# Rows of x, x1 and the adjacency renumbered so that a partition's eight rows are neighbours in memory, a third buffer for the sign masks, and a group's quotients one batch later

## What is computed

```python
x  = layernorm(x + (adj == 1) @ (x @ w1) + (adj == 2) @ (x @ w2) + (adj == 3) @ (x @ w3) + bias)
h  = x @ W.T + b
e  = (h @ we1 + be1) + (h @ we2 + be2).T          # 8192 x 8192
e  = where(e >= 0, e, 0.01 * e)
p  = softmax(where(adj > 0, e, -9e15), axis=1)
x  = layernorm(x + p @ h)
```

## Time and profile before

| | |
|---|---|
| median of 3 runs | 1608.69 us (1608.07 to 1610.11) |
| the profiled execution | 1608.2 us, of which its span is 1606.5 us |
| TensorE busy | 1435.4 us (89%) |
| VectorE busy | 1088.5 us (68%) |
| ScalarE busy | 979.4 us (61%) |
| GpSimd busy | 119.5 us (7%) |
| TensorE's mean granted clock | 0.969 of full |
| read from memory | 296.5 MB |

### The profile page before, as it was taken

How to read it: one execution, slowest core, us unless ns; L and a number is a source line. 1 busy time by engine, 2 the same in 40 slices (tenths; PEclk the granted TensorE clock), 3 DMA queues, 4 the chain that set the end, 5 groups by cost and what they waited for, 6 DMA issues and landing times.

```text
span 1606.5 us, 19366 instructions
## 1 busy us (share of the span) xinstructions
PE 1435.4 (89%) x6934; PEld 668.8 (42%) x6934; DVE 1088.5 (68%) x2432; ACT 979.4 (61%) x1536; POOL 119.5 (7%) x154
## 2 busy tenths in 40 slices
PE   1747798889999999999999988999999989998996
PEld 0323344344444444444444433444444444444443
DVE  3556677867878968778678665666566766666554
ACT  2223535555556556456555467787787887788674
POOL 3101111110101110100101030000000000000000
PEclk9988899899999999999999998999999999999998
DMA  9999999995889879967969121000000001000100
GB/s 117 125 123 118 126 98 118 112 115 69 97 108 98 98 70 121 86 69 96 84 67 115 13 66 40 8 27 27 27 27 27 27 27 52 28 27 27 34 1 15
DMA packets 124164, 109.60 MB, mean 68 GB/s; under 512 B 4960, under 2 KB 115104, under 8 KB 124064
## 3 DMA queue, kind: packets, MB, share of 16 engines
q0 software_dynamic: 67584, 67.12, 45.7%
q1 hardware_dynamic: 56480, 41.20, 9.1%
HBM read 296.49 MB, written 13.14 MB: 193 GB/s over the span
## 4 chain that ended last, share of the span: by engine, by line
PE 56%; ACT 17%; DVE 12%; DMA 11%; issue 4%; SPq 0%; DVEq 0%; ACTq 0%
PE ps L1208 35%; PE ps L1167 18%; ACT neg_masks L991 13%; DMA edges<-x 7%; DVE neg_masks L597 3%; DVE pos_masks L599 2%; DMA x_rows<-x 2%; PE ps L1176 1%; DMA e_scratch<-e_turned 1%; DMA e_row<-e_scratch 1%; PE ps L1222 1%; DVE tables L660 1%; ACT L1049 1%; PE ps L1188 1%; DVE seen L559 1%
## 5 line engine op out<-in xcount | busy, mean ns | idle before, releaser
L991 ACT ACTIVATE neg_masks<-e_row,cols 128x512 int8<-128x512 f32 x1024 | 640.4, 708 | 176.7 <-PE ps L1208 137.6
L1208 PE MATMUL ps<-pos_masks,tables 128*128 128x512 fp8e4 x2048 | 616.1, 383 | 65.6 <-DVE pos_masks L599 55.7
L1208 PE MATMUL ps<-neg_masks,tables 128*128 128x512 fp8e4 x2048 | 615.2, 382 | 0.0
L1167 PE MATMUL ps<-edge_masks,tables 128*128 128x512 fp8e4 (+1 forms) x2048 | 470.7, 389 | 0.0
L1208 PEld LDWEIGHTS ps<-pos_masks,tables 128*128 128x128 f16 x2048 | 197.1, 98 | 322.4 <-issue 93.3
L597 DVE TENSOR_TENSOR neg_masks<-pos_masks,neg_masks 128x2048 uint16<-128x2048 uint16 x128 | 156.9, 1226 | 241.9 <-ACT neg_masks L991 240.5
L1208 PEld LDWEIGHTS ps<-neg_masks,tables 128*128 128x128 f16 x2048 | 201.7, 98 | 246.8 <-issue 8.8
L1167 PEld LDWEIGHTS ps<-edge_masks,tables 128*128 128x128 f16 x2048 | 203.3, 100 | 238.1 <-issue 22.2
L578 DVE TENSOR_SCALAR edge_masks<-edges 128x512 uint16<-128x512 uint16 x512 | 123.5, 307 | 77.6 <-PE ps L1167 77.6
L982 ACT ACTIVATE edges<-ps 128x1024 uint8<-128x1024 bf16 x64 | 65.0, 1016 | 177.1 <-PE ps L1176 177.1
L599 DVE TENSOR_TENSOR pos_masks<-pos_masks,neg_masks 128x2048 uint16<-128x2048 uint16 x128 | 156.8, 1225 | 4.4
(11 more groups left out here) (128 smaller groups left out, 728.5 us busy)
## 6 DMA issues: line engine op xcount, KB each, us to landing
adj_in<-adj POOLq DMA_DIRECT2D x84, 512.0 KB, 12.0
tables<-adj POOLq DMA_DIRECT2D x28, 512.0 KB, 20.9
e_row<-e_scratch SPq DMA_DIRECT2D x34, 256.0 KB, 4.1
edges<-adj POOLq DMA_DIRECT2D x16, 512.0 KB, 12.0
part_scratch<-a_c_rows SPq DMA_DIRECT2D x18, 256.0 KB, 3.3
part_in<-part_scratch SPq DMA_DIRECT2D x18, 256.0 KB, 3.0
edges<-x SPq DMA_DIRECT2D x8, 512.0 KB, 16.2
x_rows<-x SPq DMA_DIRECT2D x8, 512.0 KB, 4.9
```

The source lines that it names most:

```text
L991: ins = e.activation(GN[:, n:n + GR].bitcast(I8), e1row[:, q % 2, :], ACT.Sign, bias=t2[:, JC * c + j:JC * c + j + 1])
L1167: ins = e.matmul(ps[:, h, :], v_hl[:, i, JC * c + j, :], U0[:, n:n + GR].bitcast(kind), start=c == 0 and j == 0 and i == 0, stop=c == NCH ...
L1208: ins = e.matmul(z_bank(q, k), tab[:, c, 2 * k + i, j, :], mask[:, n:n + GR].bitcast(F8A), start=first and j == 0 and i == 0, stop=final a ...
```

## The change

Three things are changed.

**Row numbers.** Before, partition p of a block held rows p, p+128, ..., p+896. After, it holds rows 8p to 8p+7. Loads and stores of x, x1 and the output then move 4 KB (a block) or 2 KB (a group) in one piece for each partition, where they moved 512 B pieces. The adjacency's pieces stay 4 KB in memory and 1 KB in the core, 512 a half; a partition's four rows now lie 32 KB apart and neighbouring partitions 256 KB, where it was 4 MB and 32 KB. To number the columns in the same way, `convert` reads the packed bytes with a step of eight bytes.

**Three gate buffers.** From batch 51 on the gates rotate over three buffers; the third lies in `y_turned`, which is free by then. Gates of batch m then wait for batch m-3. The spread edges keep two buffers.

**Quotients.** `quotients`, `statistics2` and `rs2_of` on VectorE and `sd2_of` and `out_of` on ScalarE stand one batch later each, and `v2` has two buffers.

```diff
-AFTER = 8
+AFTER = 9
+ROOM = max(m for m in range(NB) if SLOTS[m] <= K + START) + 3
+GATE = [m % 2 if m < ROOM else (2, (ROOM - 2) % 2, (ROOM - 1) % 2)[(m - ROOM) % 3] for m in range(NB)]
+HELD = [max([p for p in range(m) if GATE[p] == GATE[m]], default=None) for m in range(NB)]
...
+        gate_bufs = [GN[:, 0:4096], GN[:, 4096:8192],
+                     yT[:, :, :].rearrange("p h i -> p (h i)").bitcast(U8)]
...
+        def block_rows(a, S):
+            return a[S * SR:(S + 1) * SR, :].rearrange("(p t) f -> p t f", t=RB)
+        def group_rows(a, g):
+            return block_rows(a, g // 2)[:, GT * (g % 2):GT * (g % 2 + 1), :]
...
-                e.dma_start(x_in[:, v * JC:(v + 1) * JC, :], xt[:, v * JC:(v + 1) * JC, :]).then_inc(s_x, 16)
+                e.dma_start(x_in[:, v * JC:(v + 1) * JC, :], block_rows(x, v)).then_inc(s_x, 16)
...
-                e.dma_start(x1_dram[S * SR:(S + 1) * SR, :].rearrange("(t p) f -> p t f", p=P), X1[:, :, :])\
+                e.dma_start(block_rows(x1_dram, S), X1[:, :, :]).then_inc(s_x1st, 16)
...
-                            adj[r:r + GR, c * CC:(c + 1) * CC].rearrange("(b p) c -> p b c", p=P))\
+                            block_rows(adj, S)[:, GT * h:GT * (h + 1), c * CC:(c + 1) * CC])\
...
-                ge(e, s_out, f)
+                ge(e, s_out, f - 1)
...
             def rs2_of(f):
                 e.wait_ge(s_sd2, f + 1)
+                ge(e, s_out, f)
...
-                for q in ended(m - 3):
+                for q in ended(m - 4):
                     if q >= LOWS:
                         quotients(q - LOWS)
-                for q in ended(m - 4):
+                for q in ended(m - 5):
                     if q >= LOWS:
                         statistics2(q - LOWS)
-                for q in ended(m - 6):
+                for q in ended(m - 7):
                     if q >= LOWS:
                         rs2_of(q - LOWS)
...
-                e.activation(pkb[:, :], pk[:, :], ACT.Copy).then_inc(s_conv, 1)
+                e.activation(pkb[:, :].rearrange("p (j q) -> p j q", j=JC),
+                             pk[:, :].rearrange("p (q j) -> p j q", j=JC), ACT.Copy).then_inc(s_conv, 1)
...
             def gates(m):
-                ge(e, s_bat, m - 1)
+                if HELD[m] is not None:
+                    e.wait_ge(s_bat, HELD[m] + 1)
+                if GATE[m] == 2:
+                    e.wait_ge(s_lo, NS)
...
-                for q in ended(m - 5):
+                for q in ended(m - 6):
                     if q >= LOWS:
                         sd2_of(q - LOWS)
-                for q in ended(m - 7):
+                for q in ended(m - 8):
                     if q >= LOWS:
                         out_of(q - LOWS)
```

More of the change, by code:

```diff
@@ L156, in build @@
         num = in_raw[:, 0:4 * GT * (D + 1)].bitcast(F32).rearrange("p (t d) -> p t d", d=D + 1)
-        v2, ob0, ob1 = [in_raw[:, 4096 + 2048 * n:4096 + 2048 * (n + 1)].bitcast(F32)
-                        .rearrange("p (t d) -> p t d", d=D) for n in range(3)]
-        out_sb = [ob0, ob1]
+        v2_0, v2_1, ob0, ob1 = [in_raw[:, 4096 + 2048 * n:4096 + 2048 * (n + 1)].bitcast(F32)
+                                .rearrange("p (t d) -> p t d", d=D) for n in range(4)]
+        v2, out_sb = [v2_0, v2_1], [ob0, ob1]
         parts = sb("part_in", [P, 2, GR], F32)
@@ L328, in x_piece @@
             def x_piece(v):
-                e.dma_start(x_in[:, v * JC:(v + 1) * JC, :], xt[:, v * JC:(v + 1) * JC, :]).then_inc(s_x, 16)
+                e.dma_start(x_in[:, v * JC:(v + 1) * JC, :], block_rows(x, v)).then_inc(s_x, 16)
             def xg_load(S):
-                e.dma_start(xg[:, :, :], x[S * SR:(S + 1) * SR, :].rearrange("(t p) f -> p t f", p=P))\
-                    .then_inc(s_xg, 16)
+                e.dma_start(xg[:, :, :], block_rows(x, S)).then_inc(s_xg, 16)
             x_piece(0)
@@ L388, in x1_load @@
                 e.wait_ge(s_x1st, 16 * (f // 2 + 1))
-                e.dma_start(x1_in[f % 2], x1_dram[f * GR:(f + 1) * GR, :].rearrange("(t p) f -> p t f", p=P))\
-                    .then_inc(s_x1i[f % 2], 16)
+                e.dma_start(x1_in[f % 2], group_rows(x1_dram, f)).then_inc(s_x1i[f % 2], 16)
             def store(f):
                 e.wait_ge(s_out, f + 1)
-                e.dma_start(out[f * GR:(f + 1) * GR, :].rearrange("(t p) f -> p t f", p=P), out_sb[f % 2])\
-                    .then_inc(s_store[f % 2], 16)
+                e.dma_start(group_rows(out, f), out_sb[f % 2]).then_inc(s_store[f % 2], 16)
             def x1_again(n):
@@ L399, in x1_again @@
                 e.wait_ge(s_x1st, 16 * (n + 5))
-                e.dma_start(xr[n], x1_dram[(n + 4) * SR:(n + 5) * SR, :].rearrange("(t p) f -> p t f", p=P))\
-                    .then_inc(s_xr[n], 16)
+                e.dma_start(xr[n], block_rows(x1_dram, n + 4)).then_inc(s_xr[n], 16)
             q = 0
@@ L584, in edge_masks @@
                 spread(U0[:, 4096 * h:4096 * (h + 1)], bits_of(k // NCH, k % NCH), h).then_inc(s_u0, 1)
-            def slot_of(t, m):
-                return t[:, 4096 * (m % 2):4096 * (m % 2 + 1)]
             def masks(m):
@@ L591, in masks @@
                 ge(e, s_bat, m - 1)
-                u, n = slot_of(UP, m), slot_of(GN, m)
+                u, n = UP[:, 4096 * (m % 2):4096 * (m % 2 + 1)], gate_bufs[GATE[m]]
                 spread(u, bits_of(g // 2, c), g % 2).then_inc(s_unp, 1)
@@ L708, in quotients @@
                 e.wait_ge(s_x1i[f % 2], 16 * (f // 2 + 1))
-                ge(e, s_out, f)
+                ge(e, s_out, f - 1)
                 for t in range(GT):
-                    ins = e.scalar_tensor_tensor(v2[:, t, :], num[:, t, 0:D], rd[:, t:t + 1], x1_in[f % 2][:, t, :],
+                    ins = e.scalar_tensor_tensor(v2[f % 2][:, t, :], num[:, t, 0:D], rd[:, t:t + 1], x1_in[f % 2][:, t, :],
                                                  ALU.mult, ALU.add)
@@ L717, in statistics2 @@
                 for t in range(GT):
-                    ins = e.bn_stats(st2[:, t, :], v2[:, t, :])
+                    ins = e.bn_stats(st2[:, t, :], v2[f % 2][:, t, :])
                 ins.then_inc(s_st2, 1)
@@ L989, in gates @@
                 for j in range(JC):
-                    n = 4096 * (m % 2) + GR * j
-                    ins = e.activation(GN[:, n:n + GR].bitcast(I8), e1row[:, q % 2, :], ACT.Sign,
+                    n = GR * j
+                    ins = e.activation(gate_bufs[GATE[m]][:, n:n + GR].bitcast(I8), e1row[:, q % 2, :], ACT.Sign,
                                        bias=t2[:, JC * c + j:JC * c + j + 1])
@@ L1059, in out_of @@
                 for t in range(GT):
-                    ins = e.activation(out_sb[f % 2][:, t, :], v2[:, t, :], ACT.Identity, bias=nm2[:, t:t + 1],
+                    ins = e.activation(out_sb[f % 2][:, t, :], v2[f % 2][:, t, :], ACT.Identity, bias=nm2[:, t:t + 1],
                                        scale=rs2[:, t:t + 1])
@@ L1203, in batch @@
                 e.wait_ge(s_pos, m + 1)
+                both = UP[:, 4096 * (m % 2):4096 * (m % 2 + 1)], gate_bufs[GATE[m]]
                 for j in range(JC):
-                    n = 4096 * (m % 2) + GR * j
-                    for k, mask in enumerate((UP, GN)):
+                    n = GR * j
+                    for k, mask in enumerate(both):
                         for i in range(2):
```

2 lines of the change are left out of this document (removed).

## The result

The changed kernel takes 1559.05 us (median of 4 runs, 1557.01 to 1564.86) against 1608.98 us for the kernel before on the same chip: a ratio of 0.9695 with a 95% interval of 0.9668 to 0.9722. The prediction was 1551 with a range of 1533 to 1582, so 8 us too low. The profiled execution took 1559.7 us, with a span 48.4 us shorter than in the earlier trace rows; a span of 1548.5 was predicted, so in the spans the miss is 9.6 us.

What follows compares the result with a forecast made beforehand. It took x's loading to hold the start, full TensorE the middle and the gates' loop the late stage: 1606.5 - 21 - 9 - 28 = 1548.5, plus 2.2 gives 1551 us; range 1533 to 1582.

Steps and rivals of the forecast that it cites:

- pieces of x, at chunk 8: At the start: x lands in 7 us a piece instead of 16.2, so VectorE takes chunk 8 21 us earlier.
- the rest up to batch 51: First two tails: faster stores of e1 behind x1's larger pieces give 9 us together; nothing else gained before batch 51.
- late stage: Batches 51 to 127: 42.7 us of TensorE waits removed, less 13.4 and 1 for later steps; gain 28, ends 21 to 32.
- Rival 3: At the start: x still needs 16 us a piece if queues share by bytes; 1572 or 1580 us; chance 0.12.
- Store of x1: First two tails: e1's store, queued behind fewer pieces, needs about 3.0 us; gains about 4 and 4.6, taken as 9.
- about the pace at which the next slots were worked anyway: Behind chunk 8: chunks land every 10.0 us, matching the old slots' pace, so 21 us was taken as the gain.
- whatever is won ahead of it is passed on whole: TensorE's fully busy stretch, 550 to 923 us: its length stays, so earlier gains reach the end undiminished.
- the announced end of the full-TensorE stretch: Sign to look for: TensorE's fully busy stretch ends at 890 to 896 us instead of 923.
- Third buffer: Late stage: gates may start at the end of batch m-3, removing 42.7 us if ScalarE waits for nothing else.
- Later quotients: Late stage: seven row waits behind `out_of`, groups every 30.4 us; costs 13.4 us, plus 1 in one group on VectorE.
- Under the row wait that costs nothing more: Late stage: VectorE's 7.7 us behind batch E against 6.91 adds nothing under ScalarE's row wait; 1 us in one earlier group.
- The zeros: Terms taken as 0: the adjacency's new row order, and `convert` with a step of eight bytes (bounds 0 to +10 us).

Runs made afterwards that it cites:

- the two runs: Kernel before with new row numbers alone: 1586.19 us with x1 stored in large pieces, 1593.93 us with x1 stored in the old 512 B pieces.

## Why the prediction was right, and where it was 8 us off

| term of the sum | predicted | measured |
|---|---|---|
| pieces of x, at chunk 8 | -21 | -20.5 |
| the rest up to batch 51 | -9 | -0.4 |
| late stage | -28 | -28.5 |
| behind batch 127 | 0 | +1 |
| from the span to the median | +2.2 | +1.0 |

- **Pieces of x.** Right: 6.6 us against 7 assumed, and chunk 8 at 111.0 in the announced 108 to 112. Rival 3 is out: 512 KB took 16.2 us as 64 pieces for each engine and 6.6 us as 8, under a queue as full. The Trainium skill, "DMA: Bandwidth & Descriptors", section "Queues, rings and completion order", has an engine drain a packet of some 9 to 17 descriptors before it changes the queue. The prediction read that as x staying slow, which does not follow: taking a piece as a descriptor, 64 pieces are by that page's figure at least four packets and 8 are one, an estimate, so fewer pieces should be faster by it as well. The times do not speak against the page, and in what turns the engines serve the queues no run here shows.
- **Store of x1.** About right, a little high: 7.7 us between the two runs, 9 predicted. The store of e1 took 5.05 and 4.50 us, not about 3, and the two tails gave 2.8 and 4.3 us, where 4 and 4.6 were put down.
- **The step that failed** is that chunks land at "about the pace at which the next slots were worked anyway", and with it the unsaid one that the 21 us won at chunk 8 stay won up to the stretch of full TensorE. From there on "whatever is won ahead of it is passed on whole" held: -18.8 at chunk 21, -19.1 at chunk 63. The prediction priced each wait by its own duration in the kernel before and did not ask what an earlier request meets. The row of batch 1 had gone through a gap in GpSimd's queue. Now it lands in 8.3 us instead of 4.4, and chunk 14 gives 3.8 us back; 2.3 more are lost up to chunk 16 (-16.9 to -14.5), where the matmuls at the lower clock took 1.9 longer (8.96 against 7.07). A further 2.6 go from chunk 8 to 12: these chunks lay ready before and were worked off in 40.1 us, and now VectorE waits for each up to chunk 11 (2.40 us for chunk 8), so that the pace of the loads is the pace of the slots, 42.8 us. Together that is 8.8 us, against -7.1 of the two tails in this execution and -2.1 from chunk 21 to batch 51: -0.4 in the table. With it fell the announced end of the full-TensorE stretch, 27 to 33 us earlier; it was 19.4.
- **Third buffer.** Right to 0.1 us: 545.7 us alone and with the rows.
- **Later quotients.** The place, the queue (`out_of`, store, row, gates), the number of seven and the period of 30.4 (30.6 measured) were as said, and the sum too, 14.4 against 14.1. That it is no single cause the prediction said only in passing, of VectorE's 7.7 us: "Under the row wait that costs nothing more". (Its four terms add to 7.5, which is what was measured.) It holds only while the row's wait is there. Take that away, and 7.8 of the 14.1 us stay, since the same sum repeats in each group.
- **Without the third buffer** the same edit costs 33.5 us late, as its wait then has no cover at all.
- **The zeros.** The adjacency's order costs 1.8 us (0.2 to 3.4), so the zero was close; the price of the step in `convert` in the whole kernel stays open. (The loads' pace in the prediction, 1.049 MB at 0.83 MB in 8 us, is 10.1 us and not 10.0; chunks were taken up every 9.9.) On the adjacency's distance: the table in the Trainium skill, "DMA: Bandwidth & Descriptors", section "Latency and other measured facts", by which the sum would have been up to 1555, begins at 512 KiB between rows, with 207 GB/s against 214. With 256 KB the trace shows 0.83 MB in 8 us in both orders, so no loss that this view can tell; the page has no figure for that distance.

## What to carry to other kernels

A transfer's time in the old profile belongs to its moment: before a request is moved earlier, look at what the other queues carry at the new moment, and price it by a row from a full stretch. On an in-order queue look for what newly stands ahead of a load that an engine needs next; here the store that waits for a late step could be issued one round later, and nothing else got slower. Where two waits cover each other in a loop, taking one away shows the other, so price both before you keep the edit that brings them. And try a change without each of its parts: here it was 13 us faster without the third.

## What was not expected of the hardware

- Beside a full software queue (GpSimd's) the time of a transfer went with the number of its pieces more than with its bytes: 512 KB took 16.2 us as 64 pieces of 512 B for each engine and 6.6 us as 8 pieces of 4 KB. With the software queue running empty, 64 such pieces and a row of 256 KB behind them took 4.4 us, under a full one 17.8.
- ScalarE reads bytes with a step of eight at 1.127 us for 1024 elements instead of 1.050.
- A pause of TensorE of 4.87 us cost more than itself: the granted clock from 185 to 197 us was 0.69 and 0.74, and the 32 matmuls behind the pause took 8.96 us instead of 7.07.
